# Pre-norm graph layer: the addition of x to the node rows in four parts, one edge statistic behind each

## The reference

```
h     = relu(layernorm(x))                       # over the 96 numbers, eps 1e-5
cat   = [h[src], h[dst], edge_attr]              # 256 per edge
gated = sigmoid(cat @ W_e + b_e) * softplus(cat @ W_n + b_n)
out   = x + h + segment_sum(gated, dst) / max(edge_count, 1)
```

## Time and profile before

| | us |
|---|---|
| median of 3 runs | 743.97 |
| lowest, highest | 743.11, 746.23 |
| profiled execution, its own time | 752.55 |
| its span, first to last instruction | 750.8 |
| mean granted clock of PE, share of full | 0.86 |

### The profile page before, as it was taken

The page is one execution under the profiler, slowest core; times in us unless marked ns, Lnnn a source line. Parts: engine busy times, 40 slices in busy tenths (PEclk is TensorE's granted clock), DMA queues, the critical chain, the costliest instruction groups (busy, mean ns, idle before and its releaser), DMA issues.

```text
span 750.8 us, 14670 instructions
## 1 busy us (share of the span) xinstructions
PE 565.8 (75%) x3832; PEld 537.4 (72%) x3832; DVE 552.5 (74%) x2226; ACT 525.5 (70%) x1330; POOL 542.9 (72%) x404
## 2 busy tenths in 40 slices
PE   1046578888898898888887888889869778788870
PEld 0046577788788788788777887878769778778760
DVE  5766687877877787788787787787787969776550
ACT  0056677778788787786887877878868879688540
POOL 3502238888888888888888888888887878887585
PEclk9999888977987987897898898798897979889885
DMA  7435677978979879888688797897896978867442
GB/s 194 93 80 127 168 166 152 221 153 170 208 140 199 183 156 202 160 182 200 136 201 182 148 209 161 171 210 139 195 188 137 235 143 180 192 95 145 71 49 16
DMA packets 278376, 119.40 MB, mean 159 GB/s; under 512 B 261583, under 2 KB 268824, under 8 KB 278296
## 3 DMA queue, kind: packets, MB, share of 16 engines
q1 hardware_dynamic: 228366, 83.61, 46.4%
q0 software_dynamic: 34576, 18.40, 19.7%
q10 hardware_dynamic: 15354, 16.44, 8.7%
HBM read 71.36 MB, written 48.20 MB: 159 GB/s over the span
## 4 chain that ended last, share of the span: by engine, by line
PE 48%; ACT 20%; issue 14%; DVE 7%; ACTq 4%; POOL 3%; another core or an unknown queue 2%; DMA 1%; POOLq 0%; DVEq 0%
PE pick_ps L976 20%; ACT node_out L478 10%; PE sums_ps L988 6%; PE sums_ps L989 6%; PE z_ps L1041 5%; PE z_ps L1042 4%; PE z_ps L1043 4%; POOL out L411 3%; ACTq L322 3%; PE trans_ps L1021 2%; ACT log1p L550 2%; ACT log1p L545 2%; ACT log1p L540 2%; ACT src_h L508 1%
## 5 line engine op out<-in xcount | busy, mean ns | idle before, releaser
L411 POOL DMA_INDIRECT out<-final,scatter_idx x196 | 314.3, 1604 | 89.0 <-issue 57.3
L397 POOL DMA_INDIRECT edge_x<-in_x,src_idx x196 | 226.3, 1154 | 102.0 <-issue 59.2
L976 PE MATMUL pick_ps<-onehot,node_out 128*96 x1568 | 188.6, 285 | 140.5 <-issue 71.0
L976 PEld LDWEIGHTS pick_ps<-onehot,node_out 128*96 128x96 f32 x1568 | 175.4, 197 | 163.5 <-issue 163.2
L478 ACT ACTIVATE node_out<-node_x,shift,rstd 128x96 f32<-128x96 f32 x637 | 260.8, 457 | 20.6 <-DVE onehot L777 20.6
L821 DVE TENSOR_TENSOR node_out<-node_out,node_x 128x1536 f32<-128x1536 f32 x49 | 86.3, 1760 | 108.3 <-PE pick_ps L976 98.1
L496 ACT ACTIVATE dst_t<-pick_ps 96x336 f32 x98 | 43.8, 447 | 145.8 <-PE pick_ps L976 79.2
L717 DVE BATCH_NORM_STATS2 stats<-node_x 128x6 f32<-128x96 f32 x784 | 143.0, 246 | 1.3 <-issue 1.1
L1041 PE MATMUL z_ps<-w_src,src_t 97*128 97x192 f32 x392 | 106.9, 356 | 0.0
L1042 PE MATMUL z_ps<-w_dst,dst_t 96*128 96x192 f32 x392 | 101.7, 342 | 0.0
L988 PE MATMUL sums_ps<-messages,same 128*128 128x97 f32 x392 | 98.9, 343 | 3.7 <-DVE messages L739 3.7
(11 more groups left out here) (117 smaller groups left out, 589.4 us busy)
## 6 DMA issues: line engine op xcount, KB each, us to landing
node_x<-in_x SPq DMA_DIRECT2D x48, 768.0 KB
out<-node_out SPq DMA_DIRECT2D x48, 768.0 KB
dst_across<-dst_pad ACTq DMA_DIRECT2D x49, 256.0 KB
attr<-in_edge_attr SPq DMA_DIRECT2D x48, 128.0 KB
edge_x<-in_x,src_idx POOLq DMA_INDIRECT x196
out<-final,scatter_idx POOLq DMA_INDIRECT x196
low_across<-low_pad ACTq DMA_DIRECT2D x47, 64.0 KB
node_x<-in_x SPq DMA_DIRECT2D x1, 624.0 KB
```

The source lines that it names most:

```text
L397: nc.gpsimd.indirect_dma_start(out=edge_x[i % NS][:, t, :], out_offset=None, in_=x, in_offset=bass.IndirectOffsetOnAxis(ap=src_idx[:, i * ...
L411: nc.gpsimd.indirect_dma_start(out=out, in_=final[j % FINALS][:, t, :], in_offset=None, out_offset=bass.IndirectOffsetOnAxis(ap=scatter_id ...
L976: last = nc.tensor.matmul(pick_ps[0:D, bass.ds(to[b], WINDOW)], node_out[d % NS][:, h * BLOCKS + b, :], onehot[:, bass.ds(of[b], WINDOW)], ...
```

## The change

DVE's addition of x is cut into four parts of four rows each, and the four edge statistics are put between them: part 0, statistic 0, part 1, statistic 1 and so on. Parts 0 and 1 (rows 0 to 7) wait for the first group of picks only, parts 2 and 3 for both. Each part has its own waits for the two normalisations. The wait for the gathered edge rows now stands ahead of the first part; before it stood behind the whole addition. `node_sum_done` is signalled by part 3, which now has three of the four statistics ahead of it.

```diff
+QUARTER = R // TB
...
+            def node_sum(d, lo, hi):
+                wait(dve, node_norm_done, d + 1)
+                wait(dve, dve_norm_done, d + 1)
+                wait(dve, pick_done, 2 * d + 1 + (hi > BLOCKS))
+                return nc.vector.tensor_tensor(node_out[d % NS][:, lo:hi, :], node_out[d % NS][:, lo:hi, :],
+                                               node_x[d % NS][:, lo:hi, :], ALU.add)
+
...
-                if runs_step(d):
-                    wait(dve, node_norm_done, d + 1)
-                    wait(dve, dve_norm_done, d + 1)
-                    wait(dve, pick_done, 2 * d + 2)
-                    nc.vector.tensor_tensor(node_out[d % NS][:, :, :], node_out[d % NS][:, :, :], node_x[d % NS][:, :, :],
-                                            ALU.add).then_inc(node_sum_done, 1)
                 if runs_step(i):
                     dve.wait_ge(gathered[i % NS], 16 * TB * (i // NS + 1))
-                    for r in range(TB):
+                for r in range(TB):
+                    if runs_step(d):
+                        added = node_sum(d, r * QUARTER, (r + 1) * QUARTER)
+                    if runs_step(i):
                         last = nc.vector.bn_stats(stats[:, r, :], edge_x[i % NS][:, r, :])
+                if runs_step(d):
+                    added.then_inc(node_sum_done, 1)
                 if runs_rows(i):
                     last.then_inc(stats_done, 1)
```

## The result

The changed kernel takes 709.75 us (706.24 to 715.63, 4 runs) beside 745.10 (743.11 to 746.53, 4 runs): ratio 0.952, 95% interval 0.948 to 0.957. The forecast was 741.6, range 733.0 to 748.5, most likely no difference. It is missed by 32 us. Ratios leave out executions over 1.5% slower than their kernel's fastest, the medians given beside them do not. The record does not name the chips of the first measurement; three of its four runs of before are those of the table ahead of the prediction.

What follows compares the result with a forecast made beforehand. The prediction took handovers between engines inside a step, none of them full, as the bound. Middle steps gave 0, the start 0.31 + 1.04 + 1.04 = 2.4 us, hence 741.6 us on the median; range 733.0 to 748.5.

Steps and rivals of the forecast that it cites:

- POOL and DVE: Gathers behind the addition: held less by parts, but nobody waits for POOL in the middle, 0; scatters don't hold additions, 0.
- So 46 steps give 0: Middle steps, slow and fast: DVE's earlier arrival only becomes longer waits at `count` or `rough_sq`; 0.
- If that cover were gone: Wait for gathered edge rows, now ahead of all parts: 0, since POOL gathers up to three steps ahead; otherwise additions late.
- The store signal: Behind the two late statistics: store and load issued 0.5 us earlier on SP's queue, no engine waits for either; 0.
- The start: Chunks 0 to 2, before sums run: DVE comes earlier for ACT and the chain, 0.31 + 1.04 + 1.04 = 2.4 us.
- DVE's own costs: DVE's addition: each part holds DVE 0.48 us, four parts 1.92 against 1.68, 0.24 us more per step, beside waits.
- What I expected back ahead of `count`: DVE's wait for PE's sums: idle time saved at the picks comes back here, from 26 to over 50 us.
- (1): DVE the hidden bound after all: ACT's waits for `var`, 10.2 us in all, go too; 733.4 us; 13%.
- (2): Start gives nothing, since chunk 3's picks and the clock's slow stretches come at their own time; 744.0 us; 13%.
- (3): Parts 2 and 3 wait out POOL's first gathers: 12 us slower over 24 fast steps, 756 us; 5%.
- (4): Clock's slow stretches fall on other steps: ten more cost 5 us, 747 to 749, ten fewer give as much; 10%.
- The two rules: Skill's rules: fixed cost per DVE instruction, giving 2.1 instead of 2.4 us; two-input SBUF operations and GpSimd exclude each other.

Runs made afterwards that it cites:

- e14: Kernel before with one sum over the same 1536 columns, reading one tile, in place of the addition of x: 739.14 us, 0.989.
- e11: Kernel before with its addition in two parts of 8 rows, both behind all picks, statistics behind both: 21.0 us less.
- e12: Kernel before with its addition in eight parts of two rows, all behind all picks: 28.5 us less, 0.962.
- e9: Kernel before with two of the four scatters of each batch, on chip C: 0.911.
- e13: Kernel before with its addition in four parts behind all picks and two of four scatters, on chip D: 1.0052.
- e17: Kernel before with two of four scatters, on chip E: 746 us, no faster than with all of them.
- e7: Kernel before with the signal that frees the chunk for SP's store and load some 4 us later: 14.7 us saved by the ratio.
- e5: The changed kernel once more, unaltered, against the kernel before on chip B: 0.972 (0.964 to 0.979).
- e10: The changed kernel with two of the four scatters of each batch, on chip C: 0.890 of the kernel before.
- e18: Kernel before with its addition in four parts behind all picks and two of four scatters, on chip E: 746 us.

## Why the prediction was wrong

**The step that failed** is "POOL and DVE": "An addition that runs holds a gather up. With parts and gaps it is held less, and POOL is waited for by nobody in the middle: 0." Its first half is right and now shown (e14, e11, e12). The zero is wrong: the change shortens POOL's round by 0.46 us, which with the waits that are gone makes 31.3 of the 36.9 us between the two profiled executions. On chip C POOL's round sets the pace (e9). On D and E it doesn't alone (e13, e17), and what else bounds the kernel there stays open. The reading under it was "five engines lie between 70% and 75%, none is full". POOL's 542.9 us leave out 116.5 us of 0.3-us gaps that it can't avoid; from its first scatter on it was idle 9.5 us. I looked for engines that wait for POOL, found none, and didn't ask whether POOL itself ever waits. "So 46 steps give 0" fell with it: they gave 0.91 us each in the profiled pair, and on B 21 us in all.

**"If that cover were gone"** named the next wait rightly: with POOL full and DVE earlier, DVE waits 46.5 us for the gathered rows, ahead of all four parts. I had priced it at nothing because the cover was there; the change itself used it up.

**The store signal** ("no engine waits for either: 0") was mis-priced too. Moved by 4 us the other way it gives 2% (e7): the gathers then start later in the addition and are held less.

**The start** was right in kind and size. The late-signal traces can be compared directly: ACT takes the third to sixth `log_var` at 50.81, 63.20, 75.55 and 91.59 us in before and 50.58, 61.58, 72.94 and 87.90 in e5, so 0.2, 1.6, 2.6 and 3.7 us earlier. Forecast were 0.3, 1.35 and 2.4 for the first three; the fourth, another 1.1, I left out.

**DVE's own costs** were right: 0.47 us from a part to the statistic behind it (forecast 0.48). The beginning of chunk 1 in after shows it:

```profile
52.36 0.25 DVE L831 BATCH_NORM_STATS2 stats<-edge_x 128x6 f32<-128x96 f32 x1
...
55.06 0.56 DVE L789 TENSOR_TENSOR node_out<-node_out,node_x 128x384 f32<-128x384 f32 x1 [1.81 <-PE pick_ps L983]
55.53 0.25 DVE L831 BATCH_NORM_STATS2 stats<-edge_x 128x6 f32<-128x96 f32 x1
...
56.45 0.19 DVE L840 TENSOR_TENSOR half_diff<-stats 128x20 f32<-128x20 f32 x1
...
57.31 0.22 ACT L485 ACTIVATE log_var<-var 128x20 f32<-128x20 f32 x1
```

From the third part to `half_diff` are 1.39 us (forecast 1.4, before 2.44), and ACT's 1.08 us wait for `var` is gone. What I expected back ahead of `count` (26 to over 50 us) came on B, 49.6, and not in after, 24.8, where DVE is held by the gathered rows instead.

**The rivals.** (1), DVE as a hidden bound, had the right sign, and probably a true mechanism, but a gain of that kind was seen only when POOL has slack (e10 over e9, 2.2%); its 733.4 was read from ACT's waits for `var`, which rose to 16.3 us instead of going. (2) is out. (3), parts held up by POOL, is out: the longest of 196 is 634 ns; POOL is the one that yields. (4), the clock, moved in the good direction, 0.860 to 0.901 between the profiled runs, but e9's 0.916 on the old order suggests that it follows the pace; no run holds the clock still to tell. A fifth case was missing: POOL as the bound and its gathers freed.

**The two rules.** The one on two-input operations I had used only for a rival against the change. The Trainium skill, SBUF — State Buffer, section Who interferes with whom, also says that a DVE instruction with at most one SBUF input, outside the modes that use two ports, doesn't contend with GpSimd and names `tensor_reduce` as one that never does; e14 agrees (1028 ns at most). The same section tells of a probe in which `tensor_tensor` did not stall DMA, and infers that it leaves alone what the generation of descriptors needs. Whichever part of a gather it is, the trace of before shows gathers by DMA held from 0.96 to 2.38 us under an addition, and the measurement decides.

## What to carry to other kernels

Add to an engine's busy time the gaps that come with every instruction, and ask for each engine when it itself waits: an engine that is 72% busy and never waits is full, even if the list of waits never names it. A long operation on VectorE with two inputs in SBUF holds up the gathers and scatters that GpSimd starts while it runs, hardly those that were there first. Where GpSimd is full and VectorE has idle time, cutting it, or moving one of the two so that they don't meet, was worth the fixed cost of more instructions; where GpSimd had slack, the cut gave nothing (e18). Measure on more than one chip before a size is trusted: the sign held in both measurements of this change, the size was 4.8 and 2.8%.

## What the runs showed of the hardware

- A one-input reduction of 1.75 us leaves gathers at 0.94 to 1.03 us (e14); so do rows with one input that write as much as they read (1.02 at most, after). An addition of 1.76 us with two inputs in SBUF makes a gather that starts under it last up to 2.38 us; a gather already under way stays at 1.02 at most, a scatter at 1.58 (before), and the addition itself is not held (1.81 at most).
- On four of five chips, signals of PE arrive 0.9 to 5 us after its records end, in before half of them 2.6 us or more; in before most of these arrive as GpSimd's second scatter of a batch ends. On the fifth there are none. The kernel before takes about the same time on both kinds (744.1 us on the fifth, 740.8 to 748.4 on the others); the changed one took 719.5 us on B, and 709.8 in the first measurement, whose trace has one.
- On two of the four, with half of the scatters taken away nothing is saved and PE's granted clock falls from some 0.87 to 0.85; on the fifth it saves 8.9%. What links these is open.
